# A decoder layer on one core: the recurrence and the cross-attention in another order

## The reference, cut to what matters

```python
x = x + delta_rule_mixer(layernorm(x))    # below
x = x + cross_attention(layernorm(x), ctx, mask)   # 16 heads of 16, softmax over 256 keys
x = x + quantised_ffn(layernorm(x))       # 704 wide, absmax scales over the whole tensor

# delta_rule_mixer, after projections, short convolutions and l2 norms, per head and chunk of 32:
inv = (I + strict_lower(kb @ k.T))^-1     # by substitution, row by row
u, w = inv @ v, inv @ kb
for chunk: ui2 = u - w @ S; o = q @ S + lower(q @ k.T) @ ui2; S = S + k.T @ ui2
stats = [mean, var, absmean, l2] of four branches       # -> gelu gate -> softmax of 4 -> mixture
o = rmsnorm(mixture * sigmoid(gelu(...))) @ Wo
```

## Time and profile before

| | |
|---|---|
| three runs | 1296.5, 1300.8, 1303.19 us; median 1300.8 us |
| profiled execution | 1304.4 us, its span 1302.6 us |
| phase cx in it | from about 290 to about 1186 us |
| busy: PE, PEld, DVE, ACT, POOL | 1073.4, 801.0, 984.7, 755.2, 637.6 us |
| granted TensorE clock, mean | 0.912 |

### The profile page before, as it was taken

The page is one execution under the profiler, slowest core; times in us unless marked ns, Lnnn a source line. Parts: engine busy times, 40 slices in busy tenths (PEclk is TensorE's granted clock), DMA queues, the critical chain, the costliest instruction groups (busy, mean ns, idle before and its releaser), DMA issues. The chain is left out here.

```text
span 1302.6 us, 27987 instructions
## 1 busy us (share of the span) xinstructions
PE 1073.4 (82%) x8553; PEld 801.0 (61%) x8626; DVE 984.7 (76%) x2955; ACT 755.2 (58%) x1456; POOL 637.6 (49%) x2360
## 2 busy tenths in 40 slices
PE   5889888675677789999999999999999877775756
PEld 4677677674565656776676677677677645433224
DVE  4898989677666867877887787787788667734985
ACT  5778878332343356656666665665665543444866
POOL 4777775304275355466556546546545643111007
PEclk9988988885576889999999999999999988997989
DMA  6666666454215233434334343343342331204006
GB/s 186 202 203 219 204 196 199 169 114 144 75 55 138 74 99 107 130 95 138 103 122 125 110 135 104 108 145 115 111 130 77 114 111 54 66 33 176 10 1 227
DMA packets 159829, 160.31 MB, mean 123 GB/s; under 512 B 65320, under 2 KB 126656, under 8 KB 159680
## 3 DMA queue, kind: packets, MB, share of 16 engines
q1 hardware_dynamic: 155552, 157.47, 39.9%
q10 hardware_dynamic: 4128, 1.05, 0.4%
HBM read 96.34 MB, written 61.87 MB: 121 GB/s over the span
## 5 line engine op out<-in xcount | busy, mean ns | idle before, releaser
L2142 DVE CUSTOM_DVE_ANT_0 x_psA<-x_psA,x_mask_q 128x256 f32<-128x256 f32 x496 | 201.1, 447 | 74.0 <-PE x_psA L1431 73.8
L1694 ACT ACTIVATE x_PT<-x_psB 128x512 f32<-128x512 f32 x240 | 143.6, 598 | 159.3 <-PE x_psB L1458 157.1
L314 DVE SCALAR_TENSOR_TENSOR a_conv<-a_ps_proj,taps,a_conv 128x253 f32<-128x253 f32 (+2 forms) x288 | 115.0, 471 | 15.0 <-ACT a_conv L381 15.0
L537 PE MATMUL a_ps_proj<-a_hT,wqkv 128*128 128x256 f32 x384 | 106.8, 427 | 9.9 <-DVE a_conv L314 6.6
L1431 PE MATMUL x_psA<-x_Ks,x_Qs 96*128 96x256 bf16 x496 | 97.3, 278 | 16.1 <-DVE x_maxima L2142 15.7
L1458 PE MATMUL x_psB<-x_Qs,x_Ks 98*128 98x256 bf16 x480 | 93.3, 275 | 7.8 <-issue 6.2
L537 PEld LDWEIGHTS a_ps_proj<-a_hT,wqkv 128*128 128x128 f32 x384 | 79.1, 217 | 29.6 <-issue 14.6
L1860 POOL TENSOR_SCALAR x_parts_q<-x_rest 128x512 bf16<-128x512 f32 x16 | 23.9, 1496 | 118.2 <-DVE x_rest L2114 118.2
L1455 PE MATMUL x_psB<-x_mask_k,x_ident_bf 128*128 128x512 bf16 x170 | 66.3, 390 | 11.5 <-ACT x_PT L1694 9.4
L1472 PE MATMUL x_psO<-x_PT,x_V 128*32 128x256 f32 x1024 | 70.9, 396 | 1.6 <-ACT x_PT L1694 1.6
L2142 DVE DVE_READ_ACCUMULATOR2_ANT x_maxima<- 128x1 f32 x512 | 72.1, 141 | 0.0
(11 more groups left out here) (383 smaller groups left out, 3225.9 us busy)
## 6 DMA issues: line engine op xcount, KB each, us to landing
scratch_keypack<-a_keypack SPq DMA_DIRECT2D x16, 768.0 KB, 3.7
c_keypack<-scratch_keypack SPq DMA_DIRECT2D x16, 768.0 KB, 4.7
x_Ks<-scratch_k_parts SPq DMA_DIRECT2D x192, 64.0 KB, 2.2
matrix<-scratch_taps_copies SPq DMA_DIRECT2D x32, 256.0 KB, 4.0
scratch_k_parts<-x_parts_k SPq DMA_DIRECT2D x32, 192.0 KB, 2.3
scratch_q_parts<-x_parts_q SPq DMA_DIRECT2D x32, 192.0 KB, 2.3
x_Qs<-scratch_q_parts SPq DMA_DIRECT2D x32, 192.0 KB, 2.9
a_x_in<-in_x SPq DMA_DIRECT2D x16, 256.0 KB, 3.7
```

The source lines that it names most:

```text
L314: nc.vector.scalar_tensor_tensor(acc, ps_proj[PROJ_BANK[p]][:, c, 0:L - j], taps[:, p, c, TAPS - 1 - j:TAPS - j], acc, ALU.mult, ALU.add). ...
L537: last = nc.tensor.matmul(ps_proj[PROJ_BANK[p]][:, o], wqkv[:, p, c, o * P:(o + 1) * P], hT[par][:, c], start=c == 0, stop=c == FC - 1)
L1694: nc.scalar.activation(PT[:, k % (2 * GROUP)], bank_B(b, k)[0], ACT.Exp, scale=XD ** -0.5).then_inc(pexp_ready, 1)
L2142: last = nc.vector.tensor_tensor_reduce(bank_A(b, k)[0][:, s], bank_A(b, k)[0][:, s], mask_q[:, t], 1.0, LOWEST, ALU.add, ALU.max, maxima[ ...
```

## The change

`C_ORDER` alone is replaced. All 208 operations are there as before, each once; their code, buffers and waits are the same, and there are still 24 turns. Of the diff a line each, since its rows tell a reader little:

```diff
-C_ORDER = [(0, "tt"), (3, "og2"), (3, "oge"), (1, "rv"), (3, "ogs"), (3, "ctxT"), (2, "tT"), (2, "tTc"), (3, "cTc"),
...
+C_ORDER = [(5, "maxT"), (4, "sA0"), (3, "og1"), (4, "sA1"), (1, "p2"), (4, "vproj"), (4, "sA2"), (3, "og2"), (3, "ctxT"),
...
+           (2, "logits"), (1, "b0"), (5, "sB5"), (4, "sA9"), (4, "st_kp"), (0, "ld_pack"), (4, "st_qp"), (4, "ld_K0"),
+           (4, "ld_Q0"), (1, "ld_vs"), (2, "ld_hT"), (8, "st_h3"), (3, "ld_x"), (4, "ld_Q1"), (3, "ld_c"), (4, "ld_K1"),
+           (5, "ld_S"), (7, "st_x2"), (1, "c0"), (5, "sB6"), (7, "tuh"), (1, "state"), (4, "sA10"), (5, "sB7"), (5, "pv0"),
...
```

More of the change, by code:

```diff
@@ L784 @@
 NVB = 2
-C_ORDER = [(0, "tt"), (3, "og2"), (3, "oge"), (1, "rv"), (3, "ogs"), (3, "ctxT"), (2, "tT"), (2, "tTc"), (3, "cTc"),
[23 rows of a table removed]
+C_ORDER = [(5, "maxT"), (4, "sA0"), (3, "og1"), (4, "sA1"), (1, "p2"), (4, "vproj"), (4, "sA2"), (3, "og2"), (3, "ctxT"),
[12 rows of a table added]
+           (1, "a1"), (2, "mixa"), (0, "invr"), (4, "mA11"), (2, "mixb"), (2, "mixc"), (3, "qrest"), (2, "mix"), (2, "osum"),
+           (2, "osum3"), (3, "klow"), (3, "rstdx"), (6, "rstdb"), (0, "invq"), (0, "invp"), (4, "mA12"), (0, "att0"),
+           (3, "qlow"), (2, "ostat"), (1, "stats"), (2, "scale"), (1, "delta"), (1, "sums0"), (0, "invb"), (4, "mA13"),
[8 rows of a table added]
 LOWEST = -3.0e38
```

## The result

The changed kernel takes **1382.8 us** (median of 4, 1374.2 to 1385.4) against 1301.1 us (median of 4): ratio 1.062, 95% interval 1.057 to 1.068. It is slower by 80 us. The forecast was slower by 15 us, 1316, with a range from 1288 to 1334.

What follows compares the result with a forecast made beforehand. TensorE bounds the steady turn of 46.88 us; after the change SyncE's loop was to take 48.3. Eleven intervals add 15.6 us to the profiled 1304.4, 1320.0, so 1316 us for the median, range 1288 to 1334.

Steps and rivals of the forecast that it cites:

- The loop out, burst, `ctxT`, `sB0`, out: Once-a-turn chain: SyncE's loads wait for `out`, TensorE's `ctxT` and `sB0` wait for the loads; 48.3 us a turn.
- the chance of 0.56 for slower: Forecast's 0.40 (1307 to 1326 us) plus 0.16 for slower by more.
- part 2: SyncE's queue: 29.4 + 1.6 + 15.4 + 1.8 + 0.1 = 48.3 us a turn, taken to decide.
- part 4: Filling and draining, the first four turns and the last five: 0, with 4 us either way.
- the burst: SyncE's row of transfers ahead of the context: 4.45 MB at 288 GB/s, 15.4 us (14.2 to 17.0).
- The clock: In rival slower by more (0.16): one longer TensorE wait drops the clock, 2 us a turn, 1323 us without the loop.
- Part 1: TensorE's waits: 2.9 us removed, 2.0 added, giving 46.0 us a turn alone; 43.85 us busy as floor.
- Part 3: ScalarE: two added table loads, 2.6 us a turn, for which it has room; nothing added.
- my first theory: At SyncE's burst: `ld_pack`'s wait for `out` heads the loop, 48.3 us a turn.

Runs made afterwards that it cites:

- e1: The changed kernel with SyncE's 14 operations in the order and stages of before, other engines keeping their new order: 1274.5 us, ratio 0.978.
- e4: The kernel of before with gelu1 moved from ahead of eB0 to behind eB1, which adds two table loads a turn: 1354.7 us, ratio 1.040.
- e10: The changed kernel with Tanh in place of Gelu in gelu1, which takes out the two added table loads: 1389.1 us, ratio 1.065.
- e13: The kernel of before with gelu1 behind eB1 and Tanh in place of Gelu in it, so without the added table loads: 1311.3 us, ratio 1.009.
- e8: The changed kernel with ld_pack moved from the head of the burst to behind st_x2, its end: 1330.6 us, ratio 1.018.
- e11: The changed kernel with ld_vs, ld_hT, st_h3, ld_x and the context's load moved ahead of ld_pack: 1389.7 us, ratio 1.071.
- e14: The changed kernel with ld_vs, ld_hT, st_h3, ld_x and ld_c moved ahead, and ld_pack moved behind st_x2: 1333.7 us, ratio 1.025.
- e15: The changed kernel with another order of SyncE alone: six operations including ld_K1 ahead of the store of q, ld_pack at the end: 1448.1 us, ratio 1.115.
- e18: The changed kernel with SyncE alone in the order in which its waits end, ld_K1 behind the store of q: 1275.6 us, ratio 0.981.
- e19: e18 with the order of before in the first two turns for the other engines: 1270.2 us, ratio 0.978.
- e12: The changed kernel with SyncE's old order and Tanh in place of Gelu in gelu1: 1273.8 us, ratio 0.980.
- e16: The changed kernel with SyncE's old order, and the order of before in the first two turns for the other engines: 1268.1 us, ratio 0.977.
- e17: The changed kernel with values, hT and x loaded for 16 of 128 partitions from the third sequence on: 1349.2 us, ratio 1.038.

## Why the prediction was right and wrong

**Right: the direction, the cause and what shows it.** The loop out, burst, `ctxT`, `sB0`, out sets the turn; the chance of 0.56 for slower was on it. Seen as forecast: SyncE waiting at `ld_pack` and then issuing in a row (with one stop of 2 us, for the store of q), `ctxT` waiting over 2 us for a DMA, the waits of `oT8` and `maxT` gone, four table loads a turn, landings of the context and of `x_shift` far above 3.3 and 1.8 us. That a later transfer stands behind the earlier ones, the rule of the Trainium skill's page "DMA: Bandwidth & Descriptors" (section on queues, rings and completion order), agrees: 8 KB take 4.3 us at the end of this burst and 1.9 in e1.

**Wrong: the sum, by a factor of five.** Forecast 48.3 us a turn, measured 53.07, and 0 for the first turns. Of the 67 us between the forecast time and the measured one, 49 lie in the eleven intervals, about three quarters of them by the burst and one quarter by the clock, and 14 in the first four. The terms of part 2 and part 4, against the trace of the changed kernel:

| term | forecast | measured |
|---|---|---|
| `ld_pack` to `ctxT` (burst 15.4, landing 1.8) | 17.2 | 20.2 to 21.3, mean 20.7 |
| `ctxT` to the start of `out` (1.6 + 29.4, less `out`'s own 2.3) | 28.7 | 28.5 to 31.4, mean 29.9 |
| start of `out` to `ld_pack` | 2.4 | 2.5 |
| the turn | 48.3 | 53.07 |
| 11 intervals | +15.6 | +64.6 |
| first four intervals | 0 | +13.8 |

- The largest miss is **the burst**. I took 4.45 MB at 288 GB/s; the profile has 5.0 MB at 248. `ld_K1`, which I left out since it stands behind the context, is in the queue before the context has landed, and so is `st_x2`; the store of q's landing holds SyncE 2 us in the middle. The rate was below both rows that I had bounded it with, 262 and 313, which were stretches of 3.5 and 4.5 us. In five pieces of some 4 us this burst ran at 190, 286, 232, 265 and 258 GB/s: low at its start and around SyncE's stop, and at the lower of my two bounds at its end. A mean over 20 us with a wait inside was the thing to price; my low end should have gone under 262.
- **The clock.** `ctxT` to `out` is 28.5 us in e1, turn after turn, and 28.5 to 31.4 here. Behind the wait for the context in the turn shown the granted clock is 0.71 for 5 us, and the context's weight loads take 0.72 us for what took 0.42. Over ten turns, three kept 1.00 in the 5 us behind the start of `ctxT` and took 28.5 to 29.0 us to `out`; the other seven had 0.50 to 0.72 and took 29.8 to 31.4. The length of the one wait doesn't decide it: after 2.94 us the clock stayed, after 1.93 it fell. I had this as a rival, priced it at 2 us a turn without the loop and wrote only "more with it"; it comes on top of the loop's own length, because the loop makes the waits, and my sum had nothing for it. It is 1.4 us a turn on the mean. The Trainium skill's page "TensorE: Matmul & The Clock Gate" (section on the HAM clock gate), idleness loses the clock, agrees in kind with these rows and with e4's.
- **The first turns**: 0 with 4 either way, measured +13.8, of which e1 keeps 4.3. I let the bounds stand on no row at all, though the engines' order in the light turns could have been walked.
- **Part 1** had 2.0 us for new waits of TensorE, and 46.0 for its own turn. e1 has 44.94, so what is new is 1.0, half of it, and by the windows that is not all waits: TensorE's whole idle time in a turn is 0.6 us, and its busy time is 44.41 where it was 43.85, my floor "under which nothing goes". Three of 409 matmul records of the turn before are missing, and whether they make up that difference is open. The 2.0 hid how much there was to win: the order of the other four engines is 2% better than before.
- **Part 3** held for the changed kernel (e10: no difference), but by luck of the place: in the order of before the same two loads cost 40 us (e4, e13).

**What did not fit my first theory.** I called the head of the loop "the wait for `out`". e8, e11, e14 and e15 show that this is one of four: the mixture (for `ld_vs`), the low parts of q, `out` and `sB15` end within some 10 us of each other, late in TensorE's turn, and each load behind any of them is bound to it. Of the lists with the stages of the change only that of e18 and e19, in which all four stand where they hold little that is needed soon, opens the loop; SyncE's old list (e1, e12, e16) does so too.

Open: how the 107 us split between data, issuing and clock is known only in part (e17 moves data alone, and the clock follows the waits). And no run here says why most turns with a wait of 2.52 us lose the clock, and a few do not.
